# An LSTM step kernel: the output is formed on GpSimd, the output gate becomes a sigmoid, h gets a constant scale, and the set-up runs in another order

## The chip, the core and the metric

The kernel runs on one core of a Trainium2 chip. The metric is the device time of one execution in microseconds (us). The names of the engines in the profile are PE (TensorE, matrix multiply), PEld (its weight loads), DVE (VectorE), ACT (ScalarE), POOL (GpSimd) and SP (SyncE, which here only issues DMAs).

## The reference

The computation is one LSTM layer over 512 positions, with a residual sum. The batch is 16 and the width 512.

```python
xW = jnp.einsum('ntd,dg->ntg', x, Wx) + b
def step(carry, xw_t):
    prev_h, prev_c = carry
    a = xw_t + prev_h @ Wh
    i = sigmoid(a[:, :Hdim]);  f = sigmoid(a[:, Hdim:2 * Hdim])
    o = sigmoid(a[:, 2 * Hdim:3 * Hdim]);  g = tanh(a[:, 3 * Hdim:])
    next_c = f * prev_c + i * g
    next_h = o * tanh(next_c)
    return ((next_h, next_c), next_h)
...
x = x + hs            # x: (16, 512, 512), all float32
```

## The kernel before

Everything is laid out with features on the 128 partitions: a position of x, h or the output is a tile of 128 partitions by 64 columns (C = 4 blocks of features, B = 16 batch rows). The 2048 gate columns are split in two halves, n = 0 and n = 1, each with the four gates of half of the features. Matrix products keep about float32 precision by splitting each float32 operand in two float16 parts, "high" and "low", after a scaling by a power of two.

**Set-up.** The weights Wx and Wh arrive by DMA in four pieces each. DVE searches each for its largest absolute value (L457), PE sums the 128 partitions' tops with a matrix of ones (L333 for Wx, L335 for the first 16 positions of x, L358 for Wh), and DVE makes the power-of-two scales of them (L462 to L465). ACT then makes the high parts (`high_of_w`, L230 and L231). The low part of Wx is placed by PE (`place_low`, L345 and L350) and fetched by ACT (`take_low`, L251), but for one piece that POOL and DVE make; the low part of Wh is made by DVE (L468 and L470). `place_bias` (L242) starts a PSUM sum with the bias, `input_part` (L366) adds x·Wx for two positions at a time, `high_of_x` (L236) and `low_of_x` (L549) split x, and `fill(t)` (L245) copies the finished input part of position t to the sum of that position.

**The loop over 512 positions.** All engines run code written out position by position; they meet only by semaphores, and each engine works in the order of its own program. For position t: PE adds h·Wh to the sum (L374 low parts, L380 high parts); DVE turns each half out of PSUM (`turn`, L572), adds pairs (L576), and hands over to ACT, which takes tanh of three gates (L300) and then of the output gate (L305). Sigmoids are made of tanh, as (tanh(a/2) + 1)/2: the weight columns of i, f and o are halved beforehand. DVE then makes the products (L585) and the new cell (L590), ACT its tanh (L310). The output gate takes a detour: POOL adds its pairs for half 0 (L209), ACT takes tanh (L305), and POOL adds 1 and multiplies by a scale (`o_gate`, L217). DVE multiplies that by tanh of the cell, once with a float16 result (`high_of_h`, L600, what PE waits for) and once in float32 (`full_h`, L604); L594 keeps the cell, and `low_of_h` (L609) makes the low part. At the end of the position DVE forms the output row (L638) from `h_feat`, the inverse scale and x, and SP writes four such rows at a time.

**Once per 16 positions (a chunk).** DVE also searches the next chunk of x (L651, four times), makes its scales in small steps (L655, L498, L501, L505, L509, L512) at positions 5 to 8 of the chunk, and splits it in pairs (`low_of_x_pair`, L555) at positions 0, 5, 6, 9 and 12 to 15; ACT makes the high parts at positions 11 to 14, after loading two scales into registers. So 14 of the 16 positions have extra DVE work at their end, right before the next `turn(0)`; positions 10 and 11 have none.

```python
                def high_of_h(n):
                    og, ct = (k.rearrange("p (c b) -> p c b", b=B) for k in (o_gate[n][:], cell_tanh[n]))
                    dve.wait_ge(h_parts_ready[n], 2 * (t + 1))
                    dve.tensor_tensor(h_halves[par][:, 2 * n:2 * n + 2, 1, :], og, ct, ALU.mult).then_inc(h_high_ready, 1)
```

DVE's order within a position is turn(0), add_three(0), turn(1), gate_products(0), add_three(1), new_cell(0), add_last(1), gate_products(1), high_of_h(0), new_cell(1), full_h(0), keep_cell(0), low_of_h(0), high_of_h(1), full_h(1), keep_cell(1), low_of_h twice for half 1, the output row, the extra work.

## Time and profile before

| | us |
|---|---|
| median of 3 runs (lowest, highest) | 1851.96 (1851.55, 1853.14) |
| the profiled execution, its own time | 1850.74 |
| its span in the trace | 1849.0 |
| DVE busy | 1742.8 (94%) |
| PE busy | 1685.8 (91%) |
| ACT busy | 1014.0 (55%) |
| POOL busy | 546.0 (30%) |

The span runs from the first instruction to the last event in the trace; the 1.7 us between the two lie outside of it. Busy times say how much an engine had to do, not whether it was waited for. Starts in the rows below are in us from the start of the span, and a row that is merged over several instructions ends in xN. Instructions of one engine are pipelined: the next may start before the one in front has ended.

### The profile page before, as it was taken

To read this page: it belongs to the slowest core of one execution; us is meant where nothing else is said; L and a number is where in the kernel's file an instruction comes from. 1 tells how busy PE (TensorE), PEld (TensorE's weight loads), DVE (VectorE), ACT (ScalarE), POOL (GpSimd) and SP (SyncE) were. 2 spreads that over 40 slices of the span, in tenths; PEclk is the share of its full clock that TensorE was granted. 3 is DMA by queue.
4 is the path that set the end of the run, shared out by engine and by line. 5 is a ranking of instruction groups with operands and counts; after the bars stand their busy time and mean duration, and the time that the engine had idled before them with its cause. 6 is when DMAs were issued, how large, how long until landed. Compare 5 with 4: busy or idle time off the path is not lost.

```text
span 1849.0 us, 106732 instructions
## 1 busy us (share of the span) xinstructions
PE 1685.8 (91%) x45152; PEld 1081.5 (58%) x45152; DVE 1742.8 (94%) x10340; ACT 1014.0 (55%) x3991; POOL 546.0 (30%) x1563
## 2 busy tenths in 40 slices
PE   4899999999999999999999999999999999999997
PEld 2555555555555555556555556555555555556555
DVE  7999999999999999999999999999999999999998
ACT  5555555555555555555555555555555555555554
POOL 1222322322322332322332322223322323322322
PEclk9999999999999999999999999999999999999999
DMA  5000000000000000000000000000000000000000
GB/s 211 17 25 21 21 26 21 21 23 24 21 21 26 21 21 26 21 21 21 27 21 21 26 21 21 21 26 21 21 26 21 21 24 24 21 21 27 18 12 15
DMA packets 39074, 49.10 MB, mean 27 GB/s; under 512 B 4416, under 2 KB 36160, under 8 KB 38592
## 3 DMA queue, kind: packets, MB, share of 16 engines
q1 hardware_dynamic: 37152, 37.77, 6.6%
q8 instruction: 353, 5.78, 1.4%
q10 hardware_dynamic: 1440, 4.49, 0.6%
q14 instruction: 129, 1.06, 0.2%
HBM read 25.46 MB, written 16.78 MB: 23 GB/s over the span
## 4 chain that ended last, share of the span: by engine, by line
DVE 82%; ACT 8%; PE 6%; issue 3%; DMA 1%; ACTq 0%; DVEq 0%
DVE turned L572 21%; DVE mailbox L576 13%; DVE products L585 11%; DVE h_halves L609 7%; ACT gates L300 7%; DVE h_halves L600 6%; DVE gates L594 5%; DVE out_ring L638 5%; DVE h_feat L604 4%; PE acc L374 4%; DVE x_halves L555 4%; DVE mailbox L590 3%; DVE x_tops L651 2%; PE acc L380 2%; DMA wx<-in_wx 1%
## 5 line engine op out<-in xcount | busy, mean ns | idle before, releaser
L374 PE MATMUL acc<-wh_low,h_halves 128*32 128x256 f16 x16384 | 719.9, 274 | 137.2 <-DVE h_halves L600 131.9
L380 PE MATMUL acc<-wh_high,h_halves 128*32 128x256 f16 x16384 | 719.6, 274 | 0.0
L374 PEld LDWEIGHTS acc<-wh_low,h_halves 128*32 128x32 f16 x16384 | 391.3, 96 | 397.1 <-DVE h_halves L600 381.7
L366 PE MATMUL x_accs<-wx_high,x_halves 128*32 128x512 f16 x8192 | 620.6, 380 | 2.5 <-DVE x_halves L549 1.4
L300 ACT ACTIVATE gates<-mailbox 128x96 f32<-128x96 f32 x1024 | 256.4, 250 | 633.2 <-DVE mailbox L576 633.2
L217 POOL TENSOR_SCALAR o_gate<-gates,scales 128x32 f32<-128x32 f32 x1024 | 373.9, 365 | 417.6 <-ACT gates L305 417.6
L572 DVE STREAM_TRANSPOSE turned<-acc 128x256 f32<-128x256 f32 x1024 | 456.2, 446 | 19.2 <-PE acc L380 19.2
L209 POOL TENSOR_TENSOR o_preact<-turned 128x32 f32<-128x32 f32 x512 | 162.9, 318 | 867.6 <-DVE turned L572 867.6
L380 PEld LDWEIGHTS acc<-wh_high,h_halves 128*32 128x32 f16 x16384 | 350.8, 95 | 105.5
L366 PE MATMUL x_accs<-wx_low,x_halves 128*32 128x512 f16 x4096 | 398.9, 380 | 0.0
L245 ACT ACTIVATE acc<-x_accs,step_mask 128x512 f32<-128x512 f32 x512 | 335.0, 654 | 0.0
L576 DVE TENSOR_TENSOR mailbox<-turned 128x96 f32<-128x96 f32 x1024 | 269.4, 263 | 17.5
L366 PEld LDWEIGHTS x_accs<-wx_high,x_halves 128*32 128x32 f16 x8192 | 216.4, 97 | 117.7 <-issue 2.4
L310 ACT ACTIVATE mailbox<-mailbox 128x32 f32<-128x32 f32 x1024 | 191.9, 187 | 164.4 <-DVE mailbox L590 164.4
L585 DVE SCALAR_TENSOR_TENSOR products<-gates 128x64 f32<-128x64 f32 x1024 | 231.4, 226 | 53.6
L609 DVE TENSOR_TENSOR h_halves<-h_feat,h_halves 128x16 f16<-128x16 f32 (+1 forms) x1536 | 232.3, 178 | 0.0
L305 ACT ACTIVATE gates<-o_preact 128x32 f32<-128x32 f32 x1024 | 232.1, 227 | 0.0
L590 DVE SCALAR_TENSOR_TENSOR mailbox<-products 128x32 f32<-128x32 f32 x1024 | 201.5, 197 | 0.0
L594 DVE SCALAR_TENSOR_TENSOR gates<-products 128x32 f32<-128x32 f32 x1024 | 189.8, 185 | 0.0
L600 DVE TENSOR_TENSOR h_halves<-o_gate,mailbox 128x32 f16<-128x32 f32 x1024 | 188.9, 184 | 0.0
L604 DVE TENSOR_TENSOR h_feat<-o_gate,mailbox 128x32 f32<-128x32 f32 x1024 | 184.4, 180 | 0.0
L366 PEld LDWEIGHTS x_accs<-wx_low,x_halves 128*32 128x32 f16 x4096 | 109.8, 97 | 111.5 <-issue 0.3
(82 smaller groups left out, 745.3 us busy)
## 6 DMA issues: line engine op xcount, KB each, us to landing
out<-out_ring SPq DMA_DIRECT2D x128, 128.0 KB, 2.1
x_ring<-in_x SPq DMA_DIRECT2D x120, 128.0 KB, 3.0
wx<-in_wx ACTq DMA_DIRECT2D x4, 512.0 KB, 8.0
wx<-in_wx SPq DMA_DIRECT2D x4, 512.0 KB, 8.0
wh<-in_wh SPq DMA_DIRECT2D x4, 512.0 KB, 16.7
wh<-in_wh ACTq DMA_DIRECT2D x4, 512.0 KB, 17.1
x_ring<-in_x SPq DMA_DIRECT2D x2, 512.0 KB, 16.5
b_rows<-in_b ACTq DMA_DIRECT2D x1, 256.0 KB, 21.3
```

Source lines behind the costliest of these rows:

```text
L217: pool.tensor_scalar(o_gate[n][:], gates[par][n][:, 4, :], 1.0, scales[following][:, 1:2], ALU.add, ALU.mult)\
L245: act.activation(acc[t % 2][:, :, 0:GL], x_acc[t // 2 % 2], ACT.Copy, scale=step_mask[:, t % 2:t % 2 + 1])\
L300: act.activation(gates[par][n][:, 1:4, :], preact[n].rearrange("p (g c) b -> p g (c b)", c=2), ACT.Tanh, scale=rescale[chunk % 2]).then_in ...
L366: last = pe.matmul(x_acc[pair % 2][32 * j:32 * j + 32], x_halves[:, pair % (CHUNK // 2), c, half], w[:, c].rearrange("p (n q) g -> p q n g ...
L374: pe.matmul(acc[par][32 * j:32 * j + 32, n, 0:GL], h_halves[1 - par][:, c, 0:2], w_low["wh"][:, c, n * Q + j], start=False, stop=False, sk ...
L380: last = pe.matmul(acc[par][32 * j:32 * j + 32, n, 0:GL], h_halves[1 - par][:, c, 1:3], w_high["wh"][:, c, n * Q + j], start=False, stop=c ...
L572: dve.transpose(turned[n][:].rearrange("p g s b -> p (g s b)"), acc[par][:, n, 0:GL]).then_inc(turned_ready, 1)
L576: dve.tensor_tensor(preact[n], turned[n][:, 0:6, 0, :], turned[n][:, 0:6, 1, :], ALU.add)\
L585: dve.scalar_tensor_tensor(products[n][:], gates[par][n][:, 2:4, :], 1.0, gates[par][n][:, 0:2, :], ALU.add, ALU.mult).then_inc(products_r ...
L594: dve.scalar_tensor_tensor(gates[1 - par][n][:, 0, :], products[n][:, 0, :], 0.5, products[n][:, 1, :], ALU.mult, ALU.add).then_inc(cell_k ...
L600: dve.tensor_tensor(h_halves[par][:, 2 * n:2 * n + 2, 1, :], og, ct, ALU.mult).then_inc(h_high_ready, 1)
L609: dve.tensor_tensor(h_halves[par][:, cs, 2, :], h_feat[par][:, cs, :], h_halves[par][:, cs, 1, :], ALU.subtract)\
```

## The change

- **The output row.** It leaves DVE. POOL now multiplies `h_feat` by a constant into `h_plain` and adds x, for each position; SP waits for POOL.
- **The output gate.** ACT takes the sigmoid of it, with a scale twice as large, and tells DVE directly; POOL's `o_gate` is gone. Before the loop ACT computes one sigmoid, ahead of all other functions.
- **The scale of h.** It is now the constant 2^13 instead of one per chunk. `high_of_h` and `full_h` become scalar_tensor_tensor instructions, (gate x 2^13) x tanh. The chunk's scale sits in the mask by which `fill` copies the input part (`masks`), so the register with the scale of the gates is loaded once.
- **The chain of scale steps in a chunk** is spread over positions 7, 8, 10 and 11 instead of 7 and 8, and ACT's `high_of_x` moves from positions 11 to 14 to positions 12 to 15, with one register load instead of two.
- **The set-up.** PE gets small products without a use (`keep_busy`, 38, 10 and 12 of them); the sum for x is asked for after three pieces of `place_low`; DVE searches the first x in two parts, the first of them ahead of the scales of Wx; ACT takes `take_low(5)` earlier and `place_bias(1)` and `high_of_x(0, 1)` after the last piece of Wh; PE's first parts for the second pair of positions come just before the last piece of Wh.

```diff
+H_SCALE = 2.0 ** 13
...
@@ gpsimd, in the loop
-                for n in range(NG):
-                    pool.wait_ge(o_ready, NG * t + n + 1)
-                    pool.tensor_scalar(o_gate[n][:], gates[par][n][:, 4, :], 1.0, scales[following][:, 1:2], ALU.add, ALU.mult)\
-                        .then_inc(h_parts_ready[n], 1)
+                if slot == 0:
+                    pool.wait_ge(out_free[half], 32 * chunk + 1)
+                x_now = x_ring[chunk % 2][:, at // 2, :].rearrange("p (c s b) -> p c s b", s=2, b=B)[:, :, at % 2, :]
+                pool.wait_ge(h_feat_ready, NG * (t + 1))
+                pool.tensor_scalar(h_plain[:], h_feat[t % 2][:], 1 / H_SCALE, None, ALU.mult).then_inc(h_plain_ready, 1)
+                pool.wait_ge(h_plain_ready, t + 1)
+                pool.tensor_tensor(out_ring[half][:, slot, :].rearrange("p (c b) -> p c b", b=B), h_plain[:], x_now, ALU.add)\
+                    .then_inc(out_ready, 1)
@@ scalar
+            act.wait_ge(ones_ready, 2)
+            act.activation(one_gate[:], ones[:, 0:1], ACT.Sigmoid)
...
+                mask = masks[t // CHUNK % 2] if t > 0 else step_mask
-                act.activation(acc[t % 2][:, :, 0:GL], x_acc[t // 2 % 2], ACT.Copy, scale=step_mask[:, t % 2:t % 2 + 1])\
+                act.activation(acc[t % 2][:, :, 0:GL], x_acc[t // 2 % 2], ACT.Copy, scale=mask[:, t % 2:t % 2 + 1])\
...
-                    act.activation(gates[par][n][:, 4, :], o_preact[n][:].rearrange("p c b -> p (c b)"), ACT.Tanh,
-                                   scale=rescale[chunk % 2]).then_inc(o_ready, 1)
+                    act.activation(gates[par][n][:, 4, :], o_preact[n][:].rearrange("p c b -> p (c b)"), ACT.Sigmoid,
+                                   scale=(rescale if t > 0 else first_rescale)[1]).then_inc(h_parts_ready[n], 1)
...
-                if at in (11, 12, 13, 14) and chunk + 1 < CHUNKS:
+                if at in (12, 13, 14, 15) and chunk + 1 < CHUNKS:
@@ tensor, set-up
+            pe.wait_ge(w_loaded["wx"][2], 32)
+            keep_busy(38)
             pe.wait_ge(tops_ready, 1)
             pe.matmul(wx_sums[:, 0:1], ones[:], tops[:, 0:1], start=True, stop=True).then_inc(sums_ready, 1)
-            pe.wait_ge(x_top_ready, 1)
-            pe.matmul(x_sums, ones_16[:], x_top[:], start=True, stop=True).then_inc(x_sum_ready, 1)
+            keep_busy(10)
...
+            pe.wait_ge(scale_step, 1)
+            keep_busy(12)
@@ vector, in the loop
-                    dve.tensor_tensor(h_halves[par][:, 2 * n:2 * n + 2, 1, :], og, ct, ALU.mult).then_inc(h_high_ready, 1)
+                    dve.scalar_tensor_tensor(h_halves[par][:, 2 * n:2 * n + 2, 1, :], og, H_SCALE, ct, ALU.mult, ALU.mult)\
+                        .then_inc(h_high_ready, 1)
...
+                    if n == 0 and t > 1:
+                        dve.wait_ge(out_ready, t - 1)
-                    dve.tensor_tensor(h_feat[par][:, 2 * n:2 * n + 2, :], og, ct, ALU.mult).then_inc(h_feat_ready, 1)
+                    dve.scalar_tensor_tensor(h_feat[par][:, 2 * n:2 * n + 2, :], og, H_SCALE, ct, ALU.mult, ALU.mult)\
+                        .then_inc(h_feat_ready, 1)
...
-                dve.scalar_tensor_tensor(out_ring[half][:, slot, :].rearrange("p (c b) -> p c b", b=B), h_feat[par][:],
-                                         inverses[following][:, 2:3].bitcast(F32), x_now, ALU.mult, ALU.add).then_inc(out_ready, 1)
...
                 elif at == 7:
-                    dve.wait_ge(scale_step, 4 * chunk + 6)
+                    dve.wait_ge(scale_step, 5 * chunk + 7)
                     x_scale_of()
-                    dve.wait_ge(scale_step, 4 * chunk + 7)
+                elif at == 8:
+                    dve.wait_ge(scale_step, 5 * chunk + 8)
                     acc_scale_of()
-                elif at == 8:
-                    dve.wait_ge(scale_step, 4 * chunk + 8)
+                elif at == 10:
+                    dve.wait_ge(scale_step, 5 * chunk + 9)
                     scales_of(later)
-                    dve.wait_ge(scale_step, 4 * chunk + 9)
-                    inverses_of(later)
+                    acc_inverse_of()
+                elif at == 11:
+                    dve.wait_ge(scale_step, 5 * chunk + 11)
+                    masks_of(later)
```

The order of instructions on an engine is that of the code. On DVE, position 7 of the first chunk ended as follows before (`cell_kept`, `scale_step` and `acc_ready` are semaphores):

```order
L609 TENSOR_TENSOR h_halves<-h_feat,h_halves 128x16 [waits h_feat_ready] x2
L638 SCALAR_TENSOR_TENSOR out_ring<-h_feat,inverses,x_ring 128x64 [waits cell_kept]
L501 TENSOR_SCALAR x_scale_bits<-x_exponent 128x1 [waits scale_step]
L505 TENSOR_SCALAR acc_scale<-x_scale_bits,scale_bits,top_scale 128x1 [waits scale_step]
L572 STREAM_TRANSPOSE turned<-acc 128x256 [waits acc_ready]
```

In the changed kernel the same place, with its own line numbers, reads:

```order
L634 SCALAR_TENSOR_TENSOR gates<-products 128x32
L653 TENSOR_TENSOR h_halves<-h_feat,h_halves 128x16 [waits h_feat_ready] x2
L533 TENSOR_SCALAR x_scale_bits<-x_exponent 128x1 [waits scale_step,cell_kept]
L612 STREAM_TRANSPOSE turned<-acc 128x256 [waits acc_ready]
L616 TENSOR_TENSOR mailbox<-turned 128x96 [waits turned_ready]
```

The output row and the second scale step have gone from between the low parts of h and the next transpose; the second scale step stands at the same place of position 8.

On ACT the end of the set-up stood so before, from the first piece of Wh (L230, L231) to the input part of position 1 (the second L245):

```order
L230 ACTIVATE wh_high<-wh,scale_bits 128x8x64
L231 ACTIVATE wh_high<-wh,half_scale 128x8x192
L251 ACTIVATE wx_low<-acc 128x1024
L236 ACTIVATE x_halves<-x_ring,scales 128x8x32
L271 ACTIVATE h_halves<-h_feat,scales 128x4x16
L272 TENSOR_LOAD inverses
L273 TENSOR_LOAD scales
L242 ACTIVATE x_accs<-b_rows 128x512 x2
...
L230 ACTIVATE wh_high<-wh,scale_bits 128x8x64
L231 ACTIVATE wh_high<-wh,half_scale 128x8x192
L245 ACTIVATE acc<-x_accs,step_mask 128x2x256
```

And now, from the first piece of Wh on (L243 and L244 are its two parts, L256 is `place_bias`, L249 `high_of_x`, L260 `fill`):

```order
L243 ACTIVATE wh_high<-wh,scale_bits 128x8x64
L244 ACTIVATE wh_high<-wh,half_scale 128x8x192
L266 ACTIVATE wx_low<-acc 128x1024
L249 ACTIVATE x_halves<-x_ring,scales 128x8x32
L286 ACTIVATE h_halves<-h_feat,h_scaling 128x4x16
...
L260 ACTIVATE acc<-x_accs,step_mask 128x2x256
L243 ACTIVATE wh_high<-wh,scale_bits 128x8x64
L244 ACTIVATE wh_high<-wh,half_scale 128x8x192
L256 ACTIVATE x_accs<-b_rows 128x512
L249 ACTIVATE x_halves<-x_ring,scales 128x8x32
L260 ACTIVATE acc<-x_accs,masks 128x2x256
```

One `place_bias` and one `high_of_x` have moved from ahead of the last piece of Wh to behind it.

On PE the set-up began with these rows before:

```order
L333 MATMUL mailbox<-tops,ones 128x1
L335 MATMUL mailbox<-x_top,ones 128x1
L345 MATMUL acc<-wx,wx_unit 128x2x64 x2
L345 MATMUL acc<-wx,wx_unit 128x2x192 x2
L350 MATMUL acc<-wx_high,minus_unit 128x512 x2
```

And now it begins with these (L349 is `keep_busy`):

```order
L349 MATMUL mailbox<-ones 128x128 x38
L355 MATMUL mailbox<-tops,ones 128x1
L349 MATMUL mailbox<-ones 128x128 x10
L366 MATMUL acc<-wx,wx_unit 128x2x64 x2
L366 MATMUL acc<-wx,wx_unit 128x2x192 x2
...
L379 MATMUL mailbox<-x_top,ones 128x1
```

The product that waits for x no longer stands ahead of the first piece of `place_low`.

## Rows read from the trace of the kernel before

**Rows 1.** The page: the chain that ended last, shares of the span by line.

```profile
DVE turned L572 21%; DVE mailbox L576 13%; DVE products L585 11%; DVE h_halves L609 7%; ACT gates L300 7%; DVE h_halves L600 6%; DVE gates L594 5%; DVE out_ring L638 5%; DVE h_feat L604 4%; PE acc L374 4%; DVE x_halves L555 4%; DVE mailbox L590 3%; DVE x_tops L651 2%; PE acc L380 2%; DMA wx<-in_wx 1%
```

**Rows 2.** Timeline: start, duration, instruction, [idle before]; turn(0) of positions 0, 3, 511.

```profile
47.85 0.45 DVE L572 STREAM_TRANSPOSE turned<-acc 128x256 f32<-128x256 f32 x1 [0.51 <-PE acc L380]
...
59.95 0.44 DVE L572 STREAM_TRANSPOSE turned<-acc 128x256 f32<-128x256 f32 x1
...
1843.47 0.45 DVE L572 STREAM_TRANSPOSE turned<-acc 128x256 f32<-128x256 f32 x1 [0.31 <-PE acc L380]
```

**Rows 3.** Timeline, second part of position 250, which has no extra work.

```profile
929.00 0.18 DVE L600 TENSOR_TENSOR h_halves<-o_gate,mailbox 128x32 f16<-128x32 f32 x1
...
929.13 0.35 POOL L217 TENSOR_SCALAR o_gate<-gates,scales 128x32 f32<-128x32 f32 x1 [0.41 <-ACT gates L305]
929.23 0.18 DVE L604 TENSOR_TENSOR h_feat<-o_gate,mailbox 128x32 f32<-128x32 f32 x1
929.24 0.62 PE L374 MATMUL acc<-wh_low,h_halves 128*32 128x256 f16 x16 [0.27 <-DVE h_halves L600]
929.33 0.18 DVE L594 SCALAR_TENSOR_TENSOR gates<-products 128x32 f32<-128x32 f32 x1
...
929.44 0.19 DVE L609 TENSOR_TENSOR h_halves<-h_feat,h_halves 128x32 f16<-128x32 f32 x1
...
929.89 0.26 DVE L609 TENSOR_TENSOR h_halves<-h_feat,h_halves 128x16 f16<-128x16 f32 x2
...
930.06 0.28 DVE L638 SCALAR_TENSOR_TENSOR out_ring<-h_feat,inverses,x_ring 128x64 f32<-128x64 f32 x1
930.14 0.61 PE L380 MATMUL acc<-wh_high,h_halves 128*32 128x256 f16 x16
...
930.58 0.45 DVE L572 STREAM_TRANSPOSE turned<-acc 128x256 f32<-128x256 f32 x1 [0.24 <-PE acc L380]
```

**Rows 4.** Timeline, DVE: turn(0) of positions 247 and 248, end of position 252.

```profile
916.51 0.44 DVE L572 STREAM_TRANSPOSE turned<-acc 128x256 f32<-128x256 f32 x1
...
920.06 0.44 DVE L572 STREAM_TRANSPOSE turned<-acc 128x256 f32<-128x256 f32 x1
...
937.27 0.35 DVE L555 SCALAR_TENSOR_TENSOR x_halves<-x_ring,scales,x_halves 128x128 f16<-128x128 f32 x1
937.59 0.45 DVE L572 STREAM_TRANSPOSE turned<-acc 128x256 f32<-128x256 f32 x1
```

**Rows 5.** Groups by line and form: count, busy us, mean ns of one, idle before.

```profile
L594 DVE SCALAR_TENSOR_TENSOR gates<-products 128x32 f32<-128x32 f32 x1024 | 189.8, 185 | 0.0
L604 DVE TENSOR_TENSOR h_feat<-o_gate,mailbox 128x32 f32<-128x32 f32 x1024 | 184.4, 180 | 0.0
...
L204 POOL TENSOR_SCALAR wx_high<-wx,scale_bits 128x512 f16<-128x512 f32 x1 | 1.6, 1562 | 13.9 <-DVE wx_unit L486 13.9
```

**Rows 6.** Timeline of the set-up: PE, the search of Wh, and ACT.

```profile
19.12 0.18 PE L335 MATMUL mailbox<-x_top,ones 128*128 128x1 bf16 x1 [2.48 <-DVE x_top L488]
...
19.22 3.75 PE L345 MATMUL acc<-wx,wx_unit 128*128 128x128 f32 x8
...
27.87 0.16 DVE L492 TENSOR_REDUCE tops<-w_tops 128x1 f32<-128x4 f32 x1
...
28.26 1.90 PE L345 MATMUL acc<-wx,wx_unit 128*128 128x128 f32 x8
...
30.43 0.28 PE L358 MATMUL mailbox<-tops,ones 128*128 128x2 f32 x2
...
31.96 0.71 ACT L230 ACTIVATE wh_high<-wh,scale_bits 128x512 f16<-128x512 f32 x1
...
35.58 1.11 ACT L242 ACTIVATE x_accs<-b_rows 128x512 f32<-128x512 f32 x2
...
41.68 0.50 ACT L236 ACTIVATE x_halves<-x_ring,scales 128x256 f16<-128x256 f32 x1
```

**Rows 7.** Busy time by stretch: PE, PEld, DVE, ACT, POOL, then the granted clock.

```profile
48.20:51.50 3.30, 3.30 (x52) 1.75 (x44) 3.16 (x20) 2.19 (x9) 0.96 (x3) 0.50 0.02 5
```

116 lines of the change are left out of this document (69 added, 47 removed).

## The prediction

> **What bounds the kernel now.** I read the chain that ended last first. It gives DVE most of the span, and 5% of it to the output row L638 [rows 1], which the change takes off DVE. That is the claim to test, because the chain follows DVE's program order wherever no wait is seen just ahead of an instruction. So I went to the loop. From turn(0) of position 0 at 47.85 to that of position 511 at 1843.47 there are 511 positions, 3.514 us each [rows 2]; set-up is 48 us and the tail 5.5 us, so the loop is 97% of the span.
>
> Next, the timeline of a position with nothing extra on DVE. There the output row starts at 930.06 and, by the pace at which DVE starts the next instruction, is out of the way after 0.20 us; yet turn(0) starts only at 930.58, after 0.24 us of idle time that PE's last product ends [rows 3]. The positions with extra work are the test of whether DVE is the limit there. Position 252 has a split of x behind the output row: 0.35 us at 937.27, so DVE is free for the next transpose about 0.09 us before that has ended (937.53), and the transpose starts at 937.59 [rows 4]. From 930.58 to 937.59 are two positions, 3.505 us each, the first without extra work and the second with it [rows 3, 4]. An equal length with and without 0.35 us of DVE work says that DVE's end of the position is not the limit. The loop is closed by h: `high_of_h(0)` at 929.00, PE from 929.24 to its sum, the transpose at 930.58, then the gates and the cell of both engines back to `high_of_h(0)` [rows 3]. From 929.24 on PE's products of this sum follow each other without a hole to speak of.
>
> **The change, part by part.**
>
> *The output row off DVE.* 512 x 0.20 us = 102 us of DVE time go. What hides it: the wait for PE, which is 0.24 us at a quiet position and about 0.06 us at position 252. Less work in front of a wait only lengthens the wait: 0 us, but for the positions where DVE really is late.
>
> *Those positions.* In each chunk position 7 has two dependent scale steps behind the output row, and lasts 920.06 - 916.51 = 3.55 us, 0.045 more than 3.505 [rows 4]. Both the missing output row and the spread of the steps remove that: 31 chunks x 0.045 = -1.4 us. Position 8 becomes that of the second step alone and 10 and 11 get short ones; each had 0.2 us of slack and more. Positions 0 to 2 last 59.95 - 47.85 = 12.10 us [rows 2] against 3 x 3.505 = 10.52: 1.58 too long. In the first of them PE had the lower clock level, 0.50 of full speed, that is 1.2 GHz [rows 7], after a stretch with little to do; in the other two DVE makes the first splits of x behind the output row. There I take 0.2 us for each of the two, and the rest of the first (about 0.8 us) as gained too, since PE's first products for the second pair now stand right before the last piece of Wh: -1.2 us, between -0.4 and -1.6.
>
> *POOL's new work.* It starts when the second `full_h` has ended, for which the L609 at 929.89 waits too. That is at about 929.86, and with an estimated 0.1 us for the semaphore (DVE to PE it is 929.18 to 929.24) POOL starts at 929.95 [rows 3]. A POOL instruction of 32 columns takes 0.35 us [rows 3] and one of 512 takes 1.562 [rows 5], so a column costs (1562 - 350) / 480 = 2.5 ns and 64 columns 0.43 us. Two of them with a semaphore between take 0.96 us and end at 930.91, that is 0.33 us into the next position, which begins at 930.58. POOL's next task, L209, can't begin before the transpose of 0.45 us has ended, so it isn't late. Even at 0.7 us each they would only eat slack of ACT's output gate. `full_h` waits for the output of two positions earlier, long done. Cost 0 us in the loop. At the end it shows: the last output row took 0.28 us on DVE, and takes 0.1 + 0.96 - 0.2 (DVE's queue ahead of it) more or less, that is +0.55 us.
>
> The GPSIMD Engine Reference of the Trainium skill (section 3.1) gives 2.6 cycles of 1.2 GHz per column for a sum of two operands, 2.2 ns; by it the sum of 64 columns takes some 0.42 us and the term stays +0.55.
>
> *The output gate without POOL.* POOL's second `o_gate` is done at 929.13 + 0.35 = 929.48 [rows 3]. The second `high_of_h`, which needs it, stands in DVE's order behind the `low_of_h` of 929.44, and DVE starts one instruction of this size about 0.1 us after another (929.23, 929.33, 929.44), so it would not start before 929.54 anyway; the first `o_gate` is done before 929.00. POOL is not on the path: 0 us. Sigmoid for tanh is one ACT instruction for another of the same shape; the order shows a single table load, ahead of the loop, so no switch between the two. 0 us.
>
> *scalar_tensor_tensor for tensor_tensor.* This is the one price on the path. `full_h(0)` at 929.23 ends at 929.41, `low_of_h(0)` starts at 929.44 as soon as it has, and PE's next group waits for that. So each ns more in `full_h` is a ns per position, 0.51 us in all; a dearer `high_of_h(0)` delays PE's first group instead, which has to be worked through before the low parts are used, so the two don't add up. A scalar_tensor_tensor of the same 32 columns takes 185 ns with both inputs in SBUF, L604 takes 180 with one of them in PSUM [rows 5]. The new form with one input in PSUM isn't in the trace. Nearest rows: 5 ns apart, in a case (two SBUF inputs) that is if anything the dearer. I take 0, with -5 and +15 ns as bounds: -2.6 to +7.7 us.
>
> *ACT's x split one position later.* It now runs in the same position in which DVE needs it. Before, two register loads came ahead of it; now one does. DVE reaches its split 0.2 us earlier than before, and may wait up to that; its end stood 0.06 us ahead of the transpose at position 252, so the result is the old moment at worst. 0 us.
>
> *Set-up.* On PE a product that waits for DVE's search of x (2.48 us idle) stood at 19.12, ahead of all of `place_low` [rows 6]; it moves behind three pieces. The first eight L345 took 3.75 us, later ones 1.90 [rows 6]: half speed at first. The added products run in what was idle time before 16 us and may bring the higher level forward. Both together put PE 1.3 + 1.85 us and more ahead. The sums of Wh ran at 30.43 behind `place_low`, though DVE's top was there at 27.87 + 0.16 [rows 6]: 2.4 us of queue, which go; the earlier scale of Wx gives about 0.35 more. ACT starts Wh at 31.96 [rows 6] and is then busy without a gap to the end of Wh, so this reaches the first turn(0): -2.75 us. Behind it, one `place_bias` (1.11 / 2 = 0.55 us) and one `high_of_x` (0.40 of its 0.50 us) [rows 6] leave ACT's way to the last piece of Wh: -0.95. Together -3.7 us. If the clock doesn't rise earlier, only 1.0 of the 2.75 comes: -1.9. If DVE keeps up everywhere: -4.5.
>
> **Sum.** -3.7 (set-up) - 1.2 (positions 0 to 2) - 1.4 (position 7) + 0.55 (tail) + 0 (the rest) = -5.75 us. The profiled execution took 1850.74 us, a span of 1849.0 and 1.74 around it, so 1844.99 after. It lies 1.22 below the median of the runs, so the median becomes 1846.2.
>
> **Rivals.**
>
> *A: the 0.20 us come off each position* (as the chain's 5% for L638 suggests). 511 x 0.20 = 102 us: 1744. Against it stands the equal length of positions with and without extra work [rows 3, 4]. 3%. A smaller form of it, a chain shorter by 5 to 15 ns per position (a cheaper `full_h`, or less disturbance by POOL in mid-position), gives -2.6 to -7.7 more: 1838 to 1843. 9%.
>
> *B: the new instructions are dearer*, by 5 to 15 ns: 1849 to 1854. 14%. At 19 ns it would be slower than before by what a measurement shows.
>
> *C, on the other side: POOL reads SBUF while DVE makes the last low parts of h, and one holds up the other.* The first POOL instruction would begin at about 929.95, and the two L609 for blocks 2 and 3 run from 929.89 to 930.15, the second from about 929.98; PE picks them up from 930.14 on [rows 3]. The second has about 0.04 us to spare. If DVE had to stand still until POOL's 0.43 us are over, PE would get it about 0.38 us late, each position: 511 x 0.38 = 194 us, 2040. The point where it decides is 0.04 us of spare time plus 0.02 (9.5 us over 511 positions). Against it: at 929.33 DVE's L594, with two SBUF inputs, starts inside POOL's 929.13 to 929.48, and takes its usual 0.18 us [rows 3], 185 ns on average whether POOL works (first half) or not (second). For it: POOL's instructions become twice as wide. 9%, with any size from 10 to 190 us.
>
> The SBUF page of the Trainium skill (SBUF — State Buffer, "Who interferes with whom") says that a DVE instruction with two SBUF inputs contends with a GpSimd instruction that reads SBUF, for an exclusive lock held for the whole instruction. By that rule it is rival C in full, 2040 us. The trace doesn't show such a block at L594.
>
> *D: the set-up gains little* (the clock stays low): 1848 to 1849. 5%.
>
> **How the numbers follow.** The forecast (within 1843.5 to 1849) has 60%, A 12%, B 14%, C 9%, D 5%. The bound of what can be told from no change is 0.2%, 3.7 us: faster is below 1848.3, slower above 1855.7. Faster: 57 of the forecast's 60, A's 12 and 1 of D: 70%. Slower: C's 9 and 2 of B: 11%. The rest, 19%, is no difference. A range of 1840.5 to 1853.5 holds the forecast, most of the small form of A, nearly all of B and D, about 85%.
>
> **What the profile of the changed kernel would show.** Right: turn(0) is idle before nearly every position, 0.24 us at those with a split and over 0.3 at the others, while in Rows 3 and 4 only the quiet position shows it; quiet positions last 3.505 us; position 7 too; the new `full_h` takes 180 to 185 ns; the first turn(0) starts near 44.1 us; the granted clock isn't 0.50 anywhere from 44 to 50. Wrong: a position of 3.31 us (A), low_of_h longer than 0.2 us or beginning late (C), `full_h` over 190 ns (B).

## The result, and the profile after

The changed kernel takes 1859.82 us (median of 6 runs, 1858.52 to 1860.08); the kernel before, on the same chip, took 1852.27 us in its 6. The ratio is 1.0039, interval 1.0029 to 1.0049: slower by 0.4%, where 0.3% faster was predicted. The profiled execution has a span of 1858.0 us against 1849.0.

The page of the changed kernel, with the rows that answer to [rows 1] and [rows 5]. Columns of a group: count, busy us, mean ns of one, idle time before it and who ended most of it.

```profile
PE 1698.8 (91%) x45212; PEld 1075.9 (58%) x45212; DVE 1688.0 (91%) x9866; ACT 1015.6 (55%) x3992; POOL 531.3 (29%) x1563
...
DVE 52%; PE 35%; ACT 8%; issue 4%; DMA 1%; ACTq 0%; DVEq 0%; POOL 0%; POOLq 0%
...
L612 DVE STREAM_TRANSPOSE turned<-acc 128x256 f32<-128x256 f32 x1024 | 458.1, 447 | 75.4 <-PE acc L404 45.5
L225 POOL TENSOR_SCALAR h_plain<-h_feat 128x64 f32<-128x64 f32 x512 | 188.7, 369 | 1036.9 <-DVE h_feat L647 1036.9
...
L653 DVE TENSOR_TENSOR h_halves<-h_feat,h_halves 128x16 f16<-128x16 f32 (+1 forms) x1536 | 258.0, 195 | 0.0
...
L640 DVE SCALAR_TENSOR_TENSOR h_halves<-gates,mailbox 128x32 f16<-128x32 f32 x1024 | 189.6, 185 | 0.0
...
L647 DVE SCALAR_TENSOR_TENSOR h_feat<-gates,mailbox 128x32 f32<-128x32 f32 x1024 | 184.3, 180 | 0.0
```

Two things stand here. The chain no longer gives DVE nearly everything: it now shows the wait for PE in front of the transpose and follows PE from there. And one group has grown: `low_of_h`, L653, has a mean of 195 ns over its two forms. Split by form (the number of columns), the 32-column one takes 192 ns as before, the 16-column ones 197 ns on average, where before they took 172. The new forms of `high_of_h` and `full_h` (L640, L647) cost nothing.

Where it is late shows in the timeline of the changed kernel, the second part of position 250, which answers to [rows 3]:

```profile
931.73 0.18 DVE L647 SCALAR_TENSOR_TENSOR h_feat<-gates,mailbox 128x32 f32<-128x32 f32 x1
...
931.94 0.32 DVE L653 TENSOR_TENSOR h_halves<-h_feat,h_halves 128x16 f16<-128x16 f32 x2
...
932.00 0.37 POOL L225 TENSOR_SCALAR h_plain<-h_feat 128x64 f32<-128x64 f32 x1 [2.02 <-DVE h_feat L647]
...
932.20 0.63 PE L404 MATMUL acc<-wh_high,h_halves 128*32 128x256 f16 x16
...
932.45 0.32 POOL L227 TENSOR_TENSOR out_ring<-h_plain,x_ring 128x64 f32<-128x64 f32 x1
...
932.66 0.45 DVE L612 STREAM_TRANSPOSE turned<-acc 128x256 f32<-128x256 f32 x1 [0.21 <-PE acc L404]
```

POOL's first row instruction starts at 932.00, inside the pair of `low_of_h`. The pair takes 0.32 us, in [rows 3] 0.26. The two instructions apart (medians over the loop): 175 ns, then 226 ns for the last one, which starts 0.04 us after POOL's; before it was 174 and 169. PE's last groups start 0.026 us later behind turn(0) than before (3.307 against 3.281 us), and the position is longer by as much.

The same kernel has its own control. At positions 0 and 8 of a chunk POOL waits for `out_free` as well, which its queue takes as an event of its own, and its row starts 0.07 us later. The timeline of position 256 (position 0 of its chunk), DVE, then POOL:

```profile
953.14 0.26 DVE L653 TENSOR_TENSOR h_halves<-h_feat,h_halves 128x16 f16<-128x16 f32 x2
953.32 0.35 DVE L596 SCALAR_TENSOR_TENSOR x_halves<-x_ring,scales,x_halves 128x128 f16<-128x128 f32 x1
953.84 0.45 DVE L612 STREAM_TRANSPOSE turned<-acc 128x256 f32<-128x256 f32 x1 [0.17 <-PE acc L404]
```

```profile
953.27 0.37 POOL L225 TENSOR_SCALAR h_plain<-h_feat 128x64 f32<-128x64 f32 x1 [2.09 <-DVE h_feat L647]
```

The pair is back at 0.26 us, and the position, from 950.33 to 953.84, lasts 3.508 us. The other 14 positions of a chunk last 3.533 (medians by position). The two instructions still run side by side for 0.13 us: here the last `low_of_h` starts 0.03 us ahead of POOL's instruction and takes 168 ns, not held up at all. So 0.07 us decide.

The set-up: busy time by stretch of the changed kernel (PE, PEld, DVE, ACT, POOL, granted clock, DMA share, GB/s), and what PE did in the last of them.

```profile
14.36:17.78 3.42, 1.67 (x24) 1.32 (x21) 3.28 (x10) 0.14 (x1) 0.00 (x0) 1.00 1.03 411
17.78:21.19 3.41, 3.05 (x8) 2.17 (x9) 3.38 (x7) 3.41 (x4) 2.98 (x2) 0.50 1.02 408
21.19:41.67 20.48, 16.53 (x149) 10.23 (x147) 19.42 (x38) 18.72 (x22) 2.73 (x1) 1.00 0.26 100
41.67:45.08 3.41, 2.87 (x36) 1.40 (x40) 2.88 (x3) 1.78 (x4) 0.00 (x0) 0.50 0.03 5
```

```profile
42.21 0.11 PEld L398 LDWEIGHTS acc<-wh_low,h_halves 128*32 128x32 f16 x4 [1.51 <-DVE wh_low L497]
...
43.04 1.07 PE L390 MATMUL x_accs<-wx_high,x_halves 128*32 128x512 f16 x8
...
45.80 0.45 DVE L612 STREAM_TRANSPOSE turned<-acc 128x256 f32<-128x256 f32 x1 [1.25 <-PE acc L404]
```

The stretch at 0.50 (1.2 GHz) that stood in the first position before [rows 7] is gone from there (position 0 lasts 3.509 us). Another one now lies at 41.67 to 45.08; it begins inside a wait, in which the weight loads stood still for 1.51 us up to 42.21. It catches PE's products for the second pair, which the change has put ahead of the last piece of Wh: 1.07 us for eight of them, against 0.60 us for the same eight at the full clock, in e3. The first turn(0) starts at 45.80, 2.05 us earlier than [rows 2], not 3.7.

### The profile page after: what moved, and what is told of

The parts are those of the page before. It is cut to its first block, busy times and chain, and to the rows that moved or that the text cites. A ratio compares the mean times of both kernels' runs of the same rounds, so it can differ in the third digit from the quotient of the medians.

```text
span 1858.0 us, 106739 instructions
## 1 busy us (share of the span) xinstructions
PE 1698.8 (91%) x45212; PEld 1075.9 (58%) x45212; DVE 1688.0 (91%) x9866; ACT 1015.6 (55%) x3992; POOL 531.3 (29%) x1563
## 4 chain that ended last, share of the span: by engine, by line
DVE 52%; PE 35%; ACT 8%; issue 4%; DMA 1%; ACTq 0%; DVEq 0%; POOL 0%; POOLq 0%
DVE turned L612 22%; PE acc L398 21%; PE acc L404 13%; DVE mailbox L616 13%; DVE products L625 11%; ACT gates L317 7%; DVE h_halves L640 3%; DMA wx<-in_wx 1%; DVE x_halves L596 1%; ACT x_halves L249 0%; DVE h_halves L653 0%; PE acc L366 0%; DVE mailbox L630 0%; DVE gates L634 0%; DVE h_feat L647 0%
## 5 line engine op out<-in xcount | busy, mean ns | idle before, releaser
L404 PE MATMUL acc<-wh_high,h_halves 128*32 128x256 f16 x16384 | 730.5, 275 | 0.0
L612 DVE STREAM_TRANSPOSE turned<-acc 128x256 f32<-128x256 f32 x1024 | 458.1, 447 | 75.4 <-PE acc L404 45.5
L225 POOL TENSOR_SCALAR h_plain<-h_feat 128x64 f32<-128x64 f32 x512 | 188.7, 369 | 1036.9 <-DVE h_feat L647 1036.9
L404 PEld LDWEIGHTS acc<-wh_high,h_halves 128*32 128x32 f16 x16384 | 341.8, 95 | 123.8
L260 ACT ACTIVATE acc<-x_accs,masks 128x512 f32<-128x512 f32 x511 | 334.4, 654 | 0.0
L653 DVE TENSOR_TENSOR h_halves<-h_feat,h_halves 128x16 f16<-128x16 f32 (+1 forms) x1536 | 258.0, 195 | 0.0
L640 DVE SCALAR_TENSOR_TENSOR h_halves<-gates,mailbox 128x32 f16<-128x32 f32 x1024 | 189.6, 185 | 0.0
L647 DVE SCALAR_TENSOR_TENSOR h_feat<-gates,mailbox 128x32 f32<-128x32 f32 x1024 | 184.3, 180 | 0.0
L227 POOL TENSOR_TENSOR out_ring<-h_plain,x_ring 128x64 f32<-128x64 f32 x512 | 168.0, 328 | 42.8
```

The source lines that it names most:

```text
L260: act.activation(acc[t % 2][:, :, 0:GL], x_acc[t // 2 % 2], ACT.Copy, scale=mask[:, t % 2:t % 2 + 1])\
L404: last = pe.matmul(acc[par][32 * j:32 * j + 32, n, 0:GL], h_halves[1 - par][:, c, 1:3], w_high["wh"][:, c, n * Q + j], start=False, stop=c ...
L612: dve.transpose(turned[n][:].rearrange("p g s b -> p (g s b)"), acc[par][:, n, 0:GL]).then_inc(turned_ready, 1)
L640: dve.scalar_tensor_tensor(h_halves[par][:, 2 * n:2 * n + 2, 1, :], og, H_SCALE, ct, ALU.mult, ALU.mult)\
L653: dve.tensor_tensor(h_halves[par][:, cs, 2, :], h_feat[par][:, cs, :], h_halves[par][:, cs, 1, :], ALU.subtract)\
```

## The experiments

The first theory was that POOL's read of SBUF holds up the last `low_of_h` (rival C, in a small form). Its rivals: that POOL's work disturbs DVE in another way (its writes, its semaphores, or the wait of `full_h` on `out_ready`), or that the missing row or the new instructions on DVE cost the 9 us.

**e1: POOL waits until the low parts are made.**

```diff
-                pool.wait_ge(h_feat_ready, NG * (t + 1))
+                pool.wait_ge(h_ready, 3 * (t + 2))
```

> GpSimd's two instructions for the output row wait for all three low parts of h, not for the float32 h; all else is as in the changed kernel. Theory (GpSimd's first instruction, which reads SBUF, holds up the last low_of_h by 57 ns, and PE's last group with it by 27 ns at 14 of 16 positions): low_of_h L653 for one block takes about 170 ns in both of its instances (mean of all L653 178 instead of 195), a position lasts 3.506 us instead of 3.533, and the time falls by about 12 us, to 1848, below the kernel before. Rival (the dearer scalar_tensor_tensor, the mask scale or the new semaphores cost the 27 ns, whatever GpSimd does): positions stay at 3.533 and the time at 1860.

1848.77 us (10 runs) beside 1851.3 of before, ratio 0.9985 (0.9976 to 0.9995). The same work begins later. The timeline of e1, end of position 250:

```profile
926.39 0.26 DVE L653 TENSOR_TENSOR h_halves<-h_feat,h_halves 128x16 f16<-128x16 f32 x2
...
926.74 0.37 POOL L225 TENSOR_SCALAR h_plain<-h_feat 128x64 f32<-128x64 f32 x1 [2.31 <-DVE h_halves L653]
...
927.08 0.45 DVE L612 STREAM_TRANSPOSE turned<-acc 128x256 f32<-128x256 f32 x1 [0.24 <-PE acc L404]
```

The pair is at 0.26 us and the positions last 3.508. A wait that begins POOL's work some 0.3 us later turns the loss into a small gain.

**e2: POOL's first instruction reads x in place of h, the second adds h** (the output then holds x times 2^13 plus the scaled h).

```diff
-                pool.tensor_scalar(h_plain[:], h_feat[t % 2][:], 1 / H_SCALE, None, ALU.mult)...
+                pool.tensor_scalar(h_plain[:], x_now, H_SCALE, None, ALU.mult)...
```

> GpSimd's first instruction reads x (x times 2^13) at the same moment and in the same size, and the second adds the unscaled h, so the output is 2^13 times too large; h's tile is then not read by GpSimd while DVE reads it. Theory (the reads of the two engines collide, whichever tiles they read): the last low_of_h stays at 226 ns and the time at 1860. Rival (both read the same tile, h_feat, and that is what collides): it falls to 169 ns and the time to about 1848.

(The second instruction adds `h_feat` in place of x.) 1859.18 us (one run); last `low_of_h` 227 ns, positions 3.533. So it isn't that both read the tile `h_feat`: reading x, another tile in SBUF, does it too.

**e3: a memset in place of the first instruction**, the second adds the scaled h and x (the output isn't scaled back).

```diff
-                pool.tensor_scalar(h_plain[:], h_feat[t % 2][:], 1 / H_SCALE, None, ALU.mult)...
+                pool.memset(h_plain[:], 0.0)...
```

> GpSimd's first instruction is a memset of h_plain, which writes as much and reads nothing, at the same moment; the second adds unscaled h and x, so the output has h 2^13 times too large. Theory (a read of GpSimd holds up DVE's two-input read): the last low_of_h takes 169 ns, a position 3.506 us, the time is about 1848. Rival (GpSimd's writes or its being active at all hold DVE up): 226 ns and 1860. The second instruction starts only after the low parts have been made (about 0.25 us after the memset starts), so it should not disturb them.

1846.87 us (one run). Its timeline, the end of position 250 (DVE and POOL rows; between them stand rows of other engines):

```profile
924.95 0.26 DVE L653 TENSOR_TENSOR h_halves<-h_feat,h_halves 128x16 f16<-128x16 f32 x2
...
924.97 0.15 POOL L225 MEMSET h_plain<- 128x64 f32 x1 [1.99 <-DVE h_feat L647]
...
925.20 0.32 POOL L227 TENSOR_TENSOR out_ring<-h_feat,x_ring 128x64 f32<-128x64 f32 x1
```

POOL's memset lies wholly inside the pair, which keeps its 0.26 us. The positions last 3.508. The semaphores are the same and the tile written is the same, so neither of them is what holds DVE up; what is gone is the read.

**e4: the last `low_of_h` takes one input from PSUM** (the tanh of the cell in place of the full h, so h's low part in block 3 is another number).

```diff
+                    whole = cell_tanh[1].rearrange(...)[:, 1:2] if first == 3 else h_feat[par][:, cs, :]
-                    dve.tensor_tensor(h_halves[par][:, cs, 2, :], h_feat[par][:, cs, :], h_halves[par][:, cs, 1, :], ALU.subtract)
+                    dve.tensor_tensor(h_halves[par][:, cs, 2, :], whole, h_halves[par][:, cs, 1, :], ALU.subtract)
```

> The last low_of_h reads tanh of the cell from PSUM in place of float32 h from SBUF, so one of its inputs is in PSUM and only one in SBUF; the low part of the last block of h, and with it the result, are not the reference's. GpSimd is as in the changed kernel. Theory (only a DVE instruction with two SBUF inputs is held up): it takes 165 to 172 ns, positions 3.506 us, time about 1848. Rival (any DVE instruction at this moment is held up by GpSimd): 220 ns or more and 1860.

1848.53 us (one run). The timeline of e4, end of position 250:

```profile
926.31 0.17 DVE L654 TENSOR_TENSOR h_halves<-h_feat,h_halves 128x16 f16<-128x16 f32 x1
926.37 0.37 POOL L225 TENSOR_SCALAR h_plain<-h_feat 128x64 f32<-128x64 f32 x1 [2.01 <-DVE h_feat L647]
926.40 0.17 DVE L654 TENSOR_TENSOR h_halves<-mailbox,h_halves 128x16 f16<-128x16 f32 x1
```

POOL reads at the same moment as in the changed kernel, and the DVE instruction takes 167 ns in place of 226. This DVE instruction is held up when both of its inputs are in SBUF, and not when one is in PSUM.

**b1: the kernel before with one more POOL instruction**, an unused multiply that reads the 64 columns of h. The other direction: nothing taken away from the kernel before, one read added.

```diff
+                pool.wait_ge(h_feat_ready, NG * (t + 1))
+                pool.tensor_scalar(unused[:], h_feat[par][:], 1.0, None, ALU.mult).then_inc(unused_ready, 1)
```

> The kernel before with one GpSimd instruction added per position: it multiplies h_feat into a tile that nobody reads, as soon as the float32 h is there; nothing else is changed. Theory: the last low_of_h takes 226 instead of 169 ns, PE's last group is 27 ns late, and at the positions where DVE has its extra work behind the output row the 57 ns push the next transpose too: 8 positions of 16 by 27 ns and 8 by about 54, in all 20 us more, 1872; 1865 if only PE's lateness counts. Rival (the collision needs something else of the change): 1852, unchanged.

1873.03 us, ratio 1.0115 (1.0097 to 1.0133). The last `low_of_h` takes 226 ns here too. The time is as expected, its split over the positions isn't: positions 0 and 9 to 15 of a chunk last 3.526 to 3.533 us, 0.02 to 0.03 more than before, though DVE has a split of x behind the output row in six of these eight; positions 1 to 8 last 3.56 to 3.60, 0.05 to 0.07 more. What exactly adds that in just these wasn't taken apart.

**e7: POOL reads 128 columns** (both time steps of x, to a tile that nobody uses; the output isn't scaled back). This tells how long the hold lasts: until POOL's instruction is over, or only while it reads.

```diff
+        wide = sb("wide", [128, 2 * F], F32)
-                pool.tensor_scalar(h_plain[:], h_feat[t % 2][:], 1 / H_SCALE, None, ALU.mult)...
+                pool.tensor_scalar(wide[:], x_ring[chunk % 2][:, at // 2, :], H_SCALE, None, ALU.mult)...
```

> GpSimd's first instruction reads 128 columns (both positions of a pair of x) instead of 64, at the same moment; the second adds the unscaled h and x, so h in the output is 2^13 times too large. If DVE is held up only while GpSimd reads, the last low_of_h gets longer than 226 ns by 50 to 170 ns, and the position by as much (3.58 to 3.70 us, 1885 to 1945 in all). If DVE is held up for a fixed time at the start of a GpSimd instruction, it stays 226 ns and 1860. If it is held up until GpSimd's instruction has ended, it would have ended after GpSimd's first instruction already with 64 columns, which it did not (226 ns from 0.04 us after the start of one of 368 ns).

1882.06 us (one run). End of position 250 in its timeline:

```profile
941.93 0.37 DVE L654 TENSOR_TENSOR h_halves<-h_feat,h_halves 128x16 f16<-128x16 f32 x2
941.99 0.53 POOL L226 TENSOR_SCALAR wide<-x_ring 128x128 f32<-128x128 f32 x1 [2.02 <-DVE h_feat L648]
...
942.71 0.45 DVE L613 STREAM_TRANSPOSE turned<-acc 128x256 f32<-128x256 f32 x1 [0.17 <-PE acc L405]
```

The last `low_of_h` takes 279 ns: 110 more than its undisturbed 169, where 64 columns cost 57 more. That is 0.83 to 0.89 ns for each column that POOL reads, while POOL's instruction lasts 368 and 530 ns. The hold grows with the columns read and is 15 to 21% of POOL's instruction; it doesn't last until that ends. Positions: 3.587, and 3.508 again at 0 and 8. DVE loses 0.110 us and the position 0.079; the 0.03 us between them were spare.

Position 0 of a chunk confirms both the size and the moment. The timeline of e7 at the end of position 256 (DVE and POOL rows):

```profile
963.45 0.26 DVE L654 TENSOR_TENSOR h_halves<-h_feat,h_halves 128x16 f16<-128x16 f32 x2
963.58 0.53 POOL L226 TENSOR_SCALAR wide<-x_ring 128x128 f32<-128x128 f32 x1 [2.09 <-DVE h_feat L648]
963.63 0.38 DVE L597 SCALAR_TENSOR_TENSOR x_halves<-x_ring,scales,x_halves 128x128 f16<-128x128 f32 x1
```

The pair, which started ahead of POOL's instruction, isn't held up. The split behind it, also with two SBUF inputs, starts 0.05 us after POOL's instruction and takes 384 ns (median); in the changed kernel, with the same start and 64 columns read, it takes 345, no more than the 346 of before.

The hold goes both ways. Where DVE's split of 128 columns starts about 0.08 us ahead of POOL's sum (position 12 of the changed kernel), that sum takes 448 ns instead of 320; in e1 POOL's first instruction takes 401 instead of 368 at six of the eight positions with a split. It costs nothing there: position 12 lasts 3.533 us as its neighbours do, and e1's positions with a split last 3.508 as the others do.

| kernel | POOL reads | last `low_of_h` | position | us |
|---|---|---|---|---|
| e1 | 64, later | 168 ns | 3.508 | 1848.77 |
| e3 | none | 168 | 3.508 | 1846.87 |
| e4 | 64, DVE input in PSUM | 167 | 3.508 | 1848.53 |
| changed | 64 | 226 | 3.533 | 1859.82 |
| e2 | 64 of x | 227 | 3.533 | 1859.18 |
| e7 | 128 | 279 | 3.587 | 1882.06 |

**e5: the output row back on DVE**, all else as in the changed kernel.

```diff
-                pool.tensor_scalar(h_plain[:], ...); pool.tensor_tensor(out_ring[...], h_plain[:], x_now, ALU.add)
+                dve.scalar_tensor_tensor(out_ring[half][:, slot, :]..., h_feat[par][:],
+                                         1 / H_SCALE, x_now, ALU.mult, ALU.add).then_inc(out_ready, 1)
```

> The output row goes back to DVE as one scalar_tensor_tensor at its old place, and GpSimd has only its sum for the output gate; all else is as in the changed kernel. Theory (DVE's 0.20 us per position were worth nothing, since the transpose waits for PE, and GpSimd's read cost 27 ns): the same as with GpSimd waiting for the low parts, 1848.8, less 0.4 us for the shorter tail and within 1 us of it. Rival (the row did cost time on DVE, and the loop without it on DVE and without the collision is faster): this kernel is slower than 1848.8 by some us, up to 1853.

1846.13 us (8 runs), ratio 0.997 (0.9959 to 0.9981), positions 3.508. So the rest of the change is worth 5 to 6 us, and the row on DVE costs nothing that the row on POOL would save. The theory had 1848.4, within 1 us: it is 2.3 us less. Even against e1, where POOL doesn't disturb, it is 2.6 us better. Of that, 1.1 us lie in e1's last chunk, most of whose positions last 3.58 us (below) against 3.508, and 0.7 in its tail, 6.14 us against 5.42; the rest isn't traced.

**e6: no `keep_busy`** (no added products on PE in the set-up).

```diff
-                for _ in range(times):
+                for _ in range(0):
```

> The changed kernel without the 60 small products on PE. Theory (they raise PE's clock level before the first pieces of Wx's low part, which set the time of the sums of Wh): the granted clock rises only near 24 us as before, the sums of Wh come 0.9 us later, the first turn(0) at about 46.7 instead of 45.8 us, and the time is 1 us longer, 1861. Rival (they do nothing for the end of the set-up): unchanged, 1860. If a lower level after idle time hits the end of the set-up at another moment, the first positions move by up to 1 us either way.

1860.68 us, ratio 1.0047 (1.0029 to 1.0065); the first turn(0) is at 47.38 instead of 45.80. The granted clock rises at 24.54 us, as late as before. PE's sums of Wh run at 30.25 instead of 28.49, ACT's first of Wh at 31.78 instead of 30.03; in the eight profiles with the added products the sums run at 27.7 to 29.4, so these bring them forward. In the time itself it doesn't show: the intervals of e6 and of the changed kernel overlap. This row of its table of stretches shows the half clock at another place, ahead of the end of the set-up:

```profile
38.20:41.61 3.41, 3.31 (x35) 1.19 (x24) 3.07 (x4) 2.90 (x4) 0.00 (x0) 0.50 0.02 5
```

**v1: e5 with more products on PE** where it waits in the set-up (24 for 12, and 24 and 18 more ahead of the pieces of Wh).

```diff
-            keep_busy(12)
+            keep_busy(24)
...
+            keep_busy(24)
...
+                if c == 2:
+                    keep_busy(18)
```

> The version with the output row back on DVE, and on PE more of the small products in its waits of the set-up: 24 instead of 12 ahead of the first input part, 24 ahead of the first fill, 18 ahead of the third piece of Wh. In the earlier runs the first turn(0) came at 44.2 to 44.4 us where PE kept its high level through the set-up and at 45.8 to 47.4 where a stretch of 3.4 us at the lower level fell into it. Theory (that level is what the set-up still loses): no stretch at 0.50 before the loop, first turn(0) at 44.2 to 44.6 us, positions of 3.508 us, and 1 to 2.5 us less than the 1846.1 of the version without them: 1844.5. Rival (the added products stand in the way of real ones, or the level falls anyway): 1846 or more.

1845.71 us (5 runs), ratio 0.9964 (0.995 to 0.9977), the fastest of all and faster than both kernels. Its stretches:

```profile
18.56:21.97 3.41, 3.41 (x9) 1.66 (x8) 3.41 (x3) 3.13 (x4) 3.41 (x2) 0.50 1.03 410
21.97:45.05 23.08, 21.32 (x257) 14.25 (x260) 21.31 (x40) 19.81 (x24) 1.72 (x1) 1.00 0.19 75
```

The second half-clock stretch is gone. The first turn(0) comes at 45.05, 1.75 us ahead of e5's 46.80, though not at the 44.2 to 44.6 expected. The theory had 1844.5. The medians of v1 and e5 differ by 0.4 us only, less than the runs can tell.

**b2: the kernel before without its output row** (the output is left empty). The direct test of rival A.

```diff
-                dve.scalar_tensor_tensor(out_ring[half][:, slot, :]..., h_feat[par][:],
-                                         inverses[following][:, 2:3].bitcast(F32), x_now, ALU.mult, ALU.add)...
-                sp.wait_ge(out_ready, first + QUARTER)
+                sp.wait_ge(h_ready, 3 * (first + QUARTER + 1))
```

> The kernel before with the output row's instruction left out (the output is zeros); SP waits for the low parts of h instead. Theory (DVE's 0.20 us per position hide in the wait for PE): positions last 3.506 us as before, position 7 loses its 0.045 us and positions 1 and 2 0.2 us each, the transpose idles 0.24 us and more at nearly all positions; 1849.5, 2 us less. Rival A (the row lies on the path, as the chain's 5% say): 511 x 0.20 = 102 us less, 1750.

1855.28 us (10 runs), ratio 1.0016 (1.0007 to 1.0025), where the theory had 1849.5. It does less and takes longer. All positions last 3.508 to 3.513 but 10 and 11, with nothing at all on DVE behind the low parts: 3.580. The chain at the end of position 250 (250 = 15 x 16 + 10) shows a piece that b3, below, doesn't have: DVEq, DVE's sequencer. Columns: start us, us, what.

```profile
931.20 0.25 PE acc L380 x8
931.45 0.03 issue
931.48 0.02 DVEq L571
931.50 0.04 issue
931.54 0.46 DVE turned L572
```

With the row gone, the wait for the kept cell (`cell_kept`) comes to stand on the transpose, together with the wait for PE's sum. The sequencer takes one of the two as an event of its own, and only then the transpose. It is the wait for PE's sum (L571), the later of the two: the cell had been kept 0.6 us before. So 0.09 us pass from PE's end to the transpose, of which 0.02 are usual.

**b3: b2 with that wait on another instruction**, the last `low_of_h`, in place of one that was already met.

```diff
+                    if first == 3:
+                        dve.wait_ge(cell_kept, NG * (t + 1))
+                    else:
+                        dve.wait_ge(h_feat_ready, NG * t + kept)
...
                 low_of_h(3, 1, 2)
-                dve.wait_ge(cell_kept, NG * (t + 1))
```

> The kernel before without its output row on DVE, as in the run b2, and with one more edit: the wait for the kept cell no longer stands by itself ahead of the next transpose, where a second wait (for PE's sum) comes to stand on the same instruction, but on the last low_of_h, in place of a wait that was already met there. DVE does the same work in the same order. (The output rows are left out: the output is not written with values.) Theory 1 (it is the second wait on one DVE instruction that costs 0.07 us at the positions with no extra work, 62 x 0.073 = 4.5 us in b2): positions 10 and 11 last 3.508 instead of 3.580, no separate semaphore event on DVE ahead of the transpose, 4.5 us less than b2 plus what position 497 to 510 lose in b2: 1849.8 to 1851.2. Theory 2 (DVE's clean end makes PE or the transpose late in another way, the semaphores have nothing to do with it): as b2, 1855.3. Theory 3 (the 0.20 us of the row come off once no wait is in the way): 1750.

1849.76 us (10 runs), ratio 0.9988 (0.9978 to 0.9997). The same end of position 250:

```profile
929.79 0.25 PE acc L380 x8
930.03 0.02 issue
930.06 0.46 DVE turned L572
```

Positions 10 and 11 last 3.509. The spans differ by 4.4 us: 62 x 0.073 = 4.5 and eleven positions of the last chunk with 0.07 each, less 0.5 that b3 lost ahead of the first turn(0) (48.04 against 47.54) and 0.25 in positions 0 to 2. The second wait is what made b2 slow. And once more: without the row, positions are no shorter than with it.

## Why the prediction was wrong, by its steps

**The step that failed** is "POOL's new work ... Cost 0 us in the loop". It costs 14 of 16 positions 0.027 us each: 447 x 0.027 = +12.1 us. Rival C had the place (the second L609, which begins when POOL does), the mechanism (a read of SBUF against a DVE instruction with two SBUF inputs) and the point from which it decides (0.04 us spare); it was set aside to 9%, and only its largest size, 194 us, was worked out. Two errors lie in that step. First, the argument "at 929.33 DVE's L594, with two SBUF inputs, starts inside POOL's 929.13 to 929.48, and takes its usual 0.18 us" looked at the wrong pair: L594 starts 0.20 us after POOL's instruction. An estimate from e7's figure per column gives a read of 32 columns some 0.03 us, so L594 came too late to meet it. An instruction that begins inside another's span isn't yet one that overlaps its reads. Second, "Cost 0 us" needs a hold shorter than the spare time, and the size of the hold was put at nothing without a row for it: DVE lost 0.057 us, the spare time was 0.03 (put at 0.04), and the difference is the 0.027 us seen.

The trace of the kernel before had rows that bear on it, on POOL's side. There the first `o_gate` takes 388 ns (median), but 316 at position 15, where it starts 0.07 us later. From the middle of position 250, then of 255:

```profile
928.28 0.26 DVE L576 TENSOR_TENSOR mailbox<-turned 128x96 f32<-128x96 f32 x1
928.33 0.39 POOL L217 TENSOR_SCALAR o_gate<-gates,scales 128x32 f32<-128x32 f32 x1 [0.40 <-ACT gates L305]
```

```profile
945.81 0.26 DVE L576 TENSOR_TENSOR mailbox<-turned 128x96 f32<-128x96 f32 x1
945.92 0.32 POOL L217 TENSOR_SCALAR o_gate<-gates,scales 128x32 f32<-128x32 f32 x1 [0.47 <-ACT gates L305]
```

L576 has two SBUF inputs and starts 0.05 us ahead of the first of these, 0.11 ahead of the second. That reads like the same hold the other way round, a few hundredths of a us deciding; no run took it apart.

One row doesn't fit so simply. `add_last(1)`, also with two SBUF inputs, takes 201 ns in the kernel before, where it starts 0.22 us behind POOL's first `o_gate`, and 186 ns in the changed one, where POOL has nothing to do then. By the reading time it should have been free. Whether that is the same contention by another way wasn't tested.

The rule of the Trainium skill that the prediction weighed (SBUF — State Buffer, "Who interferes with whom") was right in what contends with what. The traces agree on three counts: a read holds up the instruction with two SBUF inputs (226 against 169 ns), a memset doesn't (e3), and one input in PSUM takes the DVE instruction out of it (e4). A lock that lasts for the whole instruction, as the prediction applied it, is not what the runs show, and the measurement decides: DVE was held up for 57 ns beside an instruction of 368 and for 110 beside one of 530. By the rule as it was applied the time would have been 2040 us.

**The output row off DVE, 0 us:** right, from both sides. e5 puts it back and is no slower, b2 and b3 leave it out and gain nothing in any position. Rival A falls. The chain's 5% for L638 was program order, not a limit.

**scalar_tensor_tensor for tensor_tensor, 0 us:** right; `full_h` takes 180 ns as before, `high_of_h` 185. Rival B falls. **The output gate without POOL and ACT's x split, 0 us:** nothing of either shows in e5's positions, 3.508 us.

**Position 7, -1.4 us:** right. It lasts 3.534 us as its neighbours do, and 3.508 in e5, where before it was 3.55. **Positions 0 to 2, -1.2 us:** they last 3.509, 3.785 and 3.766, in all 11.06 instead of 12.10: -1.04.

**Set-up, -3.7 us:** the mechanism was right, the size was not: -2.05. The queue on PE went (sums at 28.49 instead of 30.43, ACT's first of Wh at 30.03 instead of 31.96: -1.93, 0.8 less than forecast). The lower level, 0.50 from 17.78 to 21.19 us, still lay on the first pieces of `place_low`; in e3, with the same set-up code and no such stretch, ACT's first of Wh came at 29.11, the forecast's 2.8 us earlier. Of the 0.95 behind it only 0.12 came; there the second stretch at half clock fell on PE's products that the change had put ahead of the last piece. Where the clock stayed full, in e3 and e7 with the same set-up code, the first turn(0) came at 44.39 and 44.24; the forecast said 44.1.

**Tail, +0.55 us:** 5.84 instead of 5.48, +0.36. POOL's two instructions took 0.37 and 0.32 us rather than 0.43 each; its sum of 64 columns lasts no longer than its sum of 32 (`o_preact`, 323 ns), so the 2.2 ns per column of the prediction don't show at these sizes.

**Not foreseen:** in the last chunk DVE has no work behind the low parts at most positions, and the transpose carries two waits as in b2. Eight of those positions last 3.60 to 3.61 us where the kernel before has 3.50 to 3.51. The last two last 3.65 and 4.02 us, before 3.575 each. The chain of the changed kernel ahead of the last turn(0):

```profile
1851.45 0.24 PE acc L404 x8
1851.70 0.03 issue
1851.72 0.02 DVEq L611
1851.75 0.41 issue
1852.16 0.46 DVE turned L612
```

Behind the event of the second wait stand 0.41 us in which DVE waited for nothing that the profile shows. All kernels here with the row on POOL have such a last position (4.01 to 4.02 us); in v1, whose chain shows no event there, it lasts 3.58. The second wait alone isn't it: in b2, with the event but without POOL's row, 0.05 us stand there and the position lasts 3.65. What it is stays open. Together +1.1 us.

Sum: 12.1 - 2.05 - 1.04 - 1.4 + 1.1 + 0.36 = +9.1, against 1858.0 - 1849.0 = +9.0. The profile's own signs that the prediction had named pointed to it at once: "low_of_h longer than 0.2 us" is what the last L653 shows.

## What to carry to other kernels

Work that is moved off a busy engine is not free because it is off the path: ask what it reads, at which moment, and which instruction of the path runs in just that moment. Here a POOL instruction that starts 0.04 us before a DVE instruction with two SBUF inputs costs more than all that the change gains, and the same instruction 0.07 us later (positions 0 and 8) or 0.3 us later (e1) costs nothing; a small wait in front of it is the repair. To test such a thing in a trace, look for instructions of either engine that begin a few hundredths of a us behind one of the other's, not for those that merely lie inside its span.

And the length of a position with more and with less work on an engine tells better than its share of the chain whether the engine is the limit. Before taking work away, look at what waits that work was carrying: in b2 the row had carried one that then fell on the transpose.

## What the runs showed of the hardware that was not expected

- A POOL read of 64 or 128 columns (f32) holds up a DVE instruction with two SBUF inputs by 57 or 110 ns, 0.83 to 0.89 ns a column, while the POOL instructions last 368 and 530 ns. It is held up if it starts 0.04 us behind POOL's, not if it starts 0.03 us ahead of it.
- A DVE split of 128 columns with two SBUF inputs holds up a POOL instruction in turn: 448 ns instead of 320 (changed kernel, position 12). The `o_gate` of 32 columns in the kernel before lasts 316, 346 or 388 ns depending on what DVE has just started; a mean of its lines, 365, hides that.
- A second semaphore wait on one DVE instruction cost 0.07 us though it had been met 0.6 us before, because the one still open, for PE, was taken as an event ahead of the instruction: 3.580 against 3.508 us per position (b2, b3).
- A stretch of 3.4 us at 0.50 of the clock began at 38.2 us (e6), 41.4 (e2), 41.7 (changed), 42.4 (e4), 43.6 (e5) or 48.1 (before), one of 6.8 us at 40.8 (e1), and in e3 and e7 there was none from 16 us up to the first turn(0), though e1 to e5, e7 and the changed kernel have the same set-up code. Among these the first turn(0) came at 44.2 to 44.4 us without such a stretch and at 45.5 to 46.8 with one. What puts it where, the runs don't settle; v1's added products, after which it was absent there, are one execution.
- Positions last 3.508 us in every kernel with the change in which POOL doesn't disturb, whether DVE waits long for PE (e1, 0.20 us at positions 10 and 11) or short (e5, 0.07), and 3.505 to 3.507 there in the kernel before (0.12). That is about 1 us over the loop; its cause is open.
